# The last stage of a macaron block rebuilt: two buffers for sums, parts, results and loads, bias as PE rows, two tiles to a PSUM bank

## The reference

```python
x = x + 0.5 * ffn(layernorm(x))
x = x + attention(layernorm(x))        # ends in out @ out_proj_weight.T
x = x + 0.5 * ffn(layernorm(x))

def ffn(x):                            # T = 8192 tokens, d = 256, 8 experts, k = 2
    scores = softmax(x @ W_gate)       # 7 columns
    w = top_k(scores, 2); w = w / w.sum()
    # every expert has the weights W_expert and none overflows, so that
    # moe = (w1 + w2) * (x @ W_expert.T)
    return x @ W_shared.T + moe + bias
```

## Time and profile before

| | |
|---|---|
| median of 3 runs | 1385.76 us (1383.72 to 1387.34) |
| profiled execution | 1387.56 us, of which its span is 1385.8 us |
| busy share of the span | PE 90%, DVE 85%, ACT 66%, POOL 33% |
| mean DMA rate | 126 GB/s, mean busy share of the 16 DMA engines about a half |

### The profile page before, as it was taken

One profiled execution on the slowest core, in us unless ns is written; L12 is line 12 of the kernel. 1 busy time (PEld: TensorE's weight loads), 2 busy tenths in 40 slices (PEclk: granted clock), 3 DMA queues, 4 the chain that ended last, 5 costly groups with the idle time before them and its releaser, 6 DMA issues. The chain is left out here.

```text
span 1385.8 us, 38137 instructions
## 1 busy us (share of the span) xinstructions
PE 1253.4 (90%) x9260; PEld 832.4 (60%) x9260; DVE 1174.6 (85%) x4599; ACT 908.5 (66%) x1828; POOL 457.5 (33%) x877
## 2 busy tenths in 40 slices
PE   4999999979999999999999999999999985888785
PEld 3999988855545445455454454454454534778785
DVE  4788888749999999999999999999999963777776
ACT  3666666621778777777777777787777782444442
POOL 3333333210223222222222222222222215777671
PEclk9999999985999999999999999999999997998888
DMA  3466665973445646556466465574664643444431
GB/s 110 155 229 229 227 221 212 252 213 51 76 79 107 93 90 106 84 100 108 78 102 98 83 108 87 97 103 86 99 101 80 107 119 114 157 163 147 159 136 61
DMA packets 121898, 174.11 MB, mean 126 GB/s; under 512 B 44012, under 2 KB 71788, under 8 KB 121804
## 3 DMA queue, kind: packets, MB, share of 16 engines
q1 hardware_dynamic: 121816, 173.30, 53.9%
HBM read 96.08 MB, written 76.02 MB: 124 GB/s over the span
## 5 line engine op out<-in xcount | busy, mean ns | idle before, releaser
L1000 ACT ACTIVATE b_probs<-bank 128x512 f32<-128x512 f32 x1152 | 597.5, 614 | 135.7 <-PE bank L1124 131.9
L1027 DVE CUSTOM_DVE_ANT_0 b_junk<-bank,mask 128x512 bf16<-128x512 f32 (+3 forms) x1032 | 446.8, 488 | 1.4 <-issue 1.2
L1030 DVE TENSOR_REDUCE b_pm<-bank 128x1 f32<-128x512 f32 x516 | 322.5, 684 | 19.5 <-PE bank L1101 18.5
L1143 PE MATMUL bank<-b_probs,b_vx 128*32 128x512 f32 (+3 forms) x3072 | 310.3, 499 | 4.3 <-ACT b_o L985 1.9
L1124 PE MATMUL bank<-qs,ks 50*128 50x512 f32 (+3 forms) x1056 | 293.6, 383 | 4.5 <-ACT b_probs L1000 2.4
L1101 PE MATMUL bank<-ks,qs 48*128 48x512 f32 (+3 forms) x1056 | 277.4, 390 | 10.9 <-PEq L443 6.3
L1101 PEld LDWEIGHTS bank<-ks,qs 48*128 48x128 f32 x1056 | 165.4, 193 | 134.8 <-DVE b_pm L1030 61.6
L145 POOL TENSOR_TENSOR hold_pool<-zero 128x1 f32<-128x1 f32 x192 | 37.1, 193 | 630.8 <-ACT b_probs L1000 478.0
L1124 PEld LDWEIGHTS bank<-qs,ks 50*128 50x128 f32 x1056 | 159.7, 188 | 57.4 <-ACT b_probs L1000 51.3
L960 POOL TENSOR_SCALAR_AFFINE_SELECT b_probs<-b_probs 128x512 f32<-128x512 f32 x256 | 158.0, 635 | 0.0
L1124 PE MATMUL bank<-b_qs,b_ks 50*128 50x512 f32 (+2 forms) x480 | 135.3, 379 | 2.1 <-ACT b_probs L1000 1.2
(11 more groups left out here) (104 smaller groups left out, 2051.5 us busy)
## 6 DMA issues: line engine op xcount, KB each, us to landing
scr_qk<-a_qk SPq DMA_DIRECT2D x64, 512.0 KB, 3.2
qs<-scr_qk SPq DMA_DIRECT2D x132, 128.0 KB, 4.5
ks<-scr_qk SPq DMA_DIRECT2D x132, 128.0 KB, 5.2
scr_o<-b_o SPq DMA_DIRECT2D x64, 256.0 KB, 3.3
b_qs<-scr_qk SPq DMA_DIRECT2D x66, 128.0 KB, 4.0
b_ks<-scr_qk SPq DMA_DIRECT2D x66, 128.0 KB, 4.4
a_x<-x SPq DMA_DIRECT2D x16, 512.0 KB, 3.5
scr_x<-a_x SPq DMA_DIRECT2D x16, 512.0 KB, 2.7
```

The costliest lines, as they stand in the source:

```text
L1000: act.activation(probs[:, PROB_BUF[s], h, :], score_bank(g, t, last)[:], ACT.Exp).then_inc(p_ready, 1)
L1027: ins = dve.tensor_tensor_reduce(junk[:, t % MB, off:off + w], src, mask[:, BANK - w:BANK], 1.0, 0.0, ALU.add, ALU.max, pm[:, g.buf, 0, pl ...
L1030: ins = dve.tensor_reduce(pm[:, g.buf, 1, place(h), i:i + 1], src, AX.X, ALU.max)
L1143: last = pe.matmul(o_bank[2 * D * h:2 * D * (h + 1), col:col + w], vx[g.buf][:, j, h, :], probs[:, PROB_BUF[src], h, off:off + w], start=( ...
```

## The change

Only the last stage is changed; three load helpers of the class `First` take a buffer and a semaphore as arguments. A new class `Tail` takes the place of `Experts` there.

- `x2`, `out`, `x1`, `num`, `rden`, `oh` and `ol` get two buffers each, taken in turn by the parity of the chunk, with semaphores of their own for loads and stores. `num` and `rden` of chunk c+3 are loaded once chunk c+1 is divided, x1 of c+2 once the residual sums of c are done.
- Two tiles share a PSUM bank: output projection of tile t in bank 6 + t//2, the shared product in bank 4 + t//2. The residual sum and the collecting of the shared product are then two instructions of 128x512 instead of four of 128x256.
- The bias goes into the shared product: one more matmul for a tile, a constant 2.0 matrix against a matrix `brow` that holds the high part of the halved bias in row 0 and its low part in row 1. Five instructions of DVE build the two once. `pool_xb` is gone; x2 itself is added.
- Of the four outputs of a chunk DVE does tiles 0 and 1 as before. For tiles 2 and 3 ACT scales the expert's part by the weight in place (`act_scale`), and POOL adds the collected sum one step later (`pool_outs`). In the last chunk DVE does all four.
- Orders change: POOL divides chunk c+2 after `pool_rstd(c)`; PE does one tile of the output projection ahead of the transposes and three behind; DVE starts a step with the second collect and the logits of c-2, and ends it with the first collect of c-1; ACT runs `act_normalise` whole, between tiles 2 and 3.

The core of the diff, class `Tail` first (head and tail of the streams, the new gate and the load helpers left out; the gate differs by a wait on `scaled`):

```diff
+    def pe_tile(self, pe, k, t, first):
+        n, q = k * TPC + t, k * 2 + t // 2
+        ex, sh = self.banks["X"][t % 2], self.banks["S"][t // 2]
...
+        if not (first and t < 2):
+            pe.wait_ge(self.yl_ready, n - 1)
+        if t % 2 == 0 and not first:
+            pe.wait_ge(self.acc_ready, q - 1)
...
+        pe.matmul(half, twos[:], brow[:], start=True, stop=False)
...
+    def act_scale(self, act, k, turn):
+        act.wait_ge(self.gate_chain, k * GATE_LINKS + GATE_LINKS)
+        for t in range(self.SPLIT, TPC):
+            act.activation(self.yl[turn][:, t, 0:E], self.yl[turn][:, t, 0:E], ACT.Identity, scale=self.wsum[:, t:t + 1],
+                           bias=self.ln.zero[:, 0:1]).then_inc(self.scaled, 1)
...
+    def dve_collect(self, dve, k, p, x, turn, fresh):
+        dve.wait_ge(self.sh_done, k * 2 + p + 1)
...
+        dve.scalar_tensor_tensor(out=self.acc[turn][:, two, :].rearrange("p t e -> p (t e)"), in0=self.banks["S"][p][:], scalar=0.5,
+                                 in1=x[:, two, :].rearrange("p t e -> p (t e)"), op0=ALU.mult,
+                                 op1=ALU.add).then_inc(self.acc_ready, 1)
...
+    def pool_outs(self, pool, k, turn, fresh):
+        self.out_free(pool, k, turn, fresh)
+        pool.wait_ge(self.acc_ready, k * 2 + 2)
+        for t in range(self.SPLIT, TPC):
+            pool.wait_ge(self.scaled, k * 2 + t - 1)
+            pool.tensor_tensor(self.out[turn][:, t, :], self.yl[turn][:, t, 0:E], self.acc[turn][:, t, :],
+                               ALU.add).then_inc(self.pool_out_done, 1)
```

The step of SP:

```diff
+            def step(c, parity, o_next, out3, x_next):
+                if o_next:
                     sp.wait_ge(on_ready, c * KC + 2 * KC)
-                    load_o(c + 2)
+                    load_o(c + 3, 1 - parity)
+                if out3:
+                    ffn.store(sp, io, c - 3, 1 - parity)
+                if x_next:
+                    sp.wait_ge(x2_ready, c * 2 + 2)
+                    load_x1(c + 2, parity)
```

The step of POOL:

```diff
+            def step(c, parity, out3, nxt, nxt2, first=False):
+                if out3:
+                    ffn.pool_outs(pool, c - 3, 1 - parity, isinstance(c, int) and c < 5)
                 if nxt:
-                    divide(c + 1)
-                    low(c + 1)
+                    low(c + 1, 1 - parity)
                 ln.pool_rstd(pool, c, mhalf, first)
-                ffn.pool_xb(pool, c, x2, hbias, first)
+                if nxt2:
+                    divide(c + 2, parity)
```

The step of ACT:

```diff
             def step(c, parity, prev2, prev, here, nxt):
...
+                    high(c + 1, turn)
+                if prev:
+                    for t in range(3):
+                        ffn.act_tile(act, c - 1, t, turn, fresh)
+                if here:
+                    ln.act_normalise(act, c, x2[parity], not prev)
+                if prev:
+                    ffn.act_tile(act, c - 1, 3, turn, fresh)
+                if prev2:
+                    ffn.act_scale(act, c - 2, parity)
```

The step of DVE:

```diff
             def step(c, parity, prev2, prev, here):
...
+                if prev2:
+                    ffn.dve_collect(dve, c - 2, 1, x2[parity], parity, young(4))
+                    ffn.dve_logits(dve, c - 2, parity)
                 if prev:
                     ln.dve_low(dve, c - 1)
                 if here:
-                    residual(c, (2, 3), prev)
-                    stats(c, range(TPC))
+                    for p in range(2):
+                        residual(c, p, parity, prev, prev2)
+                        stats(c, p, parity)
                     ln.dve_aggregate(dve, c, not prev)
...
+                    ffn.dve_gate(dve, c - 2, not young(3))
+                    ffn.dve_outs(dve, c - 2, parity, young(4), (0, 1))
+                if prev:
+                    ffn.dve_collect(dve, c - 1, 0, x2[turn], turn, young(3))
```

The step of PE:

```diff
                 if here:
-                    project_out(c, prev, range(2))
-                if prev:
-                    ln.pe_transpose(pe, k, ident)
+                    project_out(c, parity, prev, (0,))
+                if prev:
+                    ln.pe_transpose(pe, c - 1, ident)
                 if here:
-                    project_out(c, prev, range(2, TPC))
+                    project_out(c, parity, prev, (1, 2, 3))
```

More of the change, by code:

```diff
@@ L1243, in _ @@
             sp.wait_ge(r_stored, 16)
-            step(1, False, True, True)
-            with loop(sp, 2, NCHUNK - 2) as c:
-                step(c, True, True, True)
-            step(NCHUNK - 2, True, True, False)
-            step(NCHUNK - 1, True, False, False)
-            store(NCHUNK - 2)
-            store(NCHUNK - 1)
-            sp.wait_ge(stored, NCHUNK * 16)
+            for c in range(3):
+                step(c, c % 2, True, False, True)
+            turns(sp, 3, NCHUNK - 3, lambda c, parity: step(c, parity, True, True, True))
+            step(NCHUNK - 3, (NCHUNK - 3) % 2, False, True, True)
+            for c in range(NCHUNK - 2, NCHUNK + 2):
+                step(c, c % 2, False, True, False)
+            ffn.store(sp, io, LAST, LAST % 2, last=True)
+            for turn in range(2):
+                sp.wait_ge(ffn.stored[turn], NCHUNK * 8)
         @block.gpsimd
@@ L1329, in _ @@
+            ffn.act_exp(act, LAST)
         @block.vector
         def _(dve):
[L1331 to L1348 removed]
@@ L1350, in stats, with residual @@
-            def stats(c, tiles):
-                for t in tiles:
-                    dve.wait_ge(x2_ready, c * TPC + t + 1)
-                    ln.dve_stats(dve, c, t, x2)
+            def residual(c, p, parity, later, later2):
+                if p == 0:
+                    if parity or not (isinstance(c, int) and c == 0):
+                        dve.wait_ge(x1_loaded[parity], c * 8 + 8 * parity)
+                    else:
+                        dve.wait_ge(chunk.x1_loaded, 16)
+                    if later2:
+                        dve.wait_ge(ln.xn_ready, c * TPC - TPC)
+                dve.wait_ge(op_ready, c * TPC + 2 * p + 2)
+                two = slice(2 * p, 2 * p + 2)
+                dve.tensor_tensor(x2[parity][:, two, :].rearrange("p t e -> p (t e)"), o_bank[p][:],
+                                  x1[parity][:, two, :].rearrange("p t e -> p (t e)"), ALU.add).then_inc(x2_ready, 1)
@@ L1434, in macaron @@
+            step(0, 0, False)
+            step(1, 1, True, first=True)
+            turns(pe, 2, NCHUNK, lambda c, parity: step(c, parity, True))
+            step(NCHUNK, 0, True, here=False)
 def macaron(nc, x, wqkv_t, wsh_t, wex_t, wgate, wout_t, bias, out):
```

308 lines of the change are left out of this document (190 added, 118 removed).

## The result

| | before | after |
|---|---|---|
| median, us | 1386.05 (1383.72 to 1387.34, 4 runs) | 1350.38 (1347.45 to 1353.60, 4 runs) |
| ratio to before, 95% interval | | 0.9745 (0.9719 to 0.9771) |
| profiled execution, us | 1387.56, span 1385.8 | 1353.60, span 1351.8 |
| mean distance of the starts of `dve_low`, ten steps from 1207 or 1208 us on | 13.53 | 10.57 |

The forecast was 1350.0, so the time is met; not all of its terms are. First the table of stretches after, which answers the earlier trace rows: us long, busy us and instructions of PE, PEld, DVE, ACT and POOL, the granted clock, the DMA share, GB/s. The last row is one step.

A forecast was written before the change was run, and what follows sets the result against it. The prediction took a cycle of waits between engines to bound the last stage, no engine being full. It summed 1171.0 + 15 x 10.9 + 15.5 = 1350.0 us; forecast 1342 to 1361, with the range reaching from 1342.5 to 1370.

The forecast's parts named there:

- Path 1: Layernorm of chunk c in a steady step, residual sums to second half of `low`, ACT's scalings included: 10.5 us.
- The 0.4 us added for three paths side by side: Supplement on the steady step's paths, giving the forecast period of 10.9 us.
- Path 2: PE in a steady step: 76 matmuls, transposes, a stand for the last normalised tile; ends at 10.4 to 10.5 us.
- Path 3: DVE in a steady step: 8.65 us of work plus 1.0 to 1.5 of stands for POOL, 9.7 to 10.1.
- Rival C: Slower: blocks between DVE and POOL decide, placed at the gate; 16.3 us a step, 1432 us at worst; chance 0.08.
- The cover of the loads: POOL's `rden` load gets a whole step more; if that failed, division late by up to 2.1 us, before its cast.
- PE's stand for the residual sum: Old steady steps: PE waits for DVE to read a shared bank, 27.5 us in 13 waits; claimed to vanish.
- the two waits: Old steady steps: PE for the residual sum (27.5 us) and POOL for `rden` (14.9), seen as closing the cycle.
- Head and drain: Stage's start and end: head change counted zero (bounds -1 and +1.5 us), drain 15.5 us.
- Rival A: Stands move, PE waits for `low`, clock keeps falling: period 12.1 us, time 1368; chance 0.23 with what lies between.
- Rival B: Cycle not shortened, new work and waits eat the buffers' gain: period 13.1 to 13.3 us, 1382 to 1388; chance 0.07.

The follow-up runs named there:

- e1: Kernel after, with ACT's scaling of tiles 2 and 3 cut to one column of 256: 1344.97 us, ratio 0.9706, period 10.14.
- e13: Kernel after, with ACT's scalings of chunk c-3 moved behind the layernorm's cast of chunk c-1: 1346.64 us, ratio 0.9706, period 10.25.
- e2: Kernel after without the four bias matmuls of a chunk (bias not added): 1351.53 us, ratio 0.9765, period 10.57.
- e4: Kernel after, with POOL dividing chunk c+2 ahead of the layernorm's scale of chunk c: 1368.19 us, ratio 0.9872, period 12.04.
- e5: Kernel after, with all four outputs on DVE, without ACT's scaling and `pool_outs`: 1359.40 us, ratio 0.9812, period 11.40.
- e12: Kernel after with single buffers for `num` and `rden` alone, loaded a step later: 1378.35 us, ratio 0.9945, period 12.46.
- e7: Kernel after with single buffers for `num`, `rden`, `x1` and `out`, loads a step later: 1386.49 us, ratio 1.0006, period 13.05.
- e11: Kernel after with a single buffer for `out` alone: 1363.07 us, ratio 0.9831, period 11.55.
- e8: Kernel after with the old banks (tiles t and t+2 share), four half-width residual sums, two ahead of `low`: 1349.81 us, ratio 0.9753, period 10.81.
- e14: Kernel before with two buffers for `num`, `rden` and `out`, loads one chunk earlier, nothing else: 1382.89 us, ratio 0.9969, period 13.30.
- e6: Kernel after, with head loads of `x1` of chunk 1 and of chunk 2 issued only once chunk 1 is divided: 1354.41 us, ratio 0.9786.

## Why the prediction was right or wrong

**Path 1 was right term by term, and is the period.** From the end of one `low` to the end of the next:

| term | priced | measured |
|---|---|---|
| residual sums, statistics, aggregates | 3.36 | 1251.67 to 1255.07: 3.40 |
| POOL's four | 1.88 | to 1257.06: 1.99 |
| handing over to ACT | 0.14 | to 1257.19: 0.13 |
| four normalisations | 2.08 | to 1259.17: 1.98 |
| tile 3 | 0.27 | to 1259.44: 0.27 |
| two scalings | 1.00 | to 1260.43: 0.99 |
| casts, half of `low` | 1.77 | to 1262.23: 1.80 |
| sum | 10.5 | 10.56 |

The scaling, which before had no row for, was priced from the normalisation of the same shape, and e1 shows that all of it lies on the path: 0.42 less work, 0.43 less period.

**The 0.4 us added for three paths side by side was wrong.** No run shows such a term. The distances from start to start hold what a handing over costs already, and path 1 alone, at 10.56, is the period of 10.57. This made twelve periods 10.9 long and not 10.54: 4.3 us too many.

**Path 2** was priced 0.2 too long, and PE is not the limit in these kernels. PE's own step was priced at 10.15 and is 9.96: the transposes take 0.79 from their start to the next matmul and not their duration of 1.04. PE stands 0.34 to 0.37 for `low`. Even in e1 and e13 the period (10.14, 10.25) stays above the 9.96. The bias costs nothing in a steady step, as it lies within PE's stand (e2).

**Path 3 was priced with the blocks on the wrong engine.** The gate does lie beside POOL's small instructions and none of its own takes over 0.19. The second output and the logits were to wait 1.0 to 1.5 us. Measured are 0.88 for two outputs and 0.19 for the difference. The outputs do meet the division, and it is the division that became 0.21 longer, with room for it. The difference meets nothing: it begins as the division ends (1259.79) and is done before POOL's outputs (1260.11). DVE's own work was right: of the step of 10.57 it stands 1.05 for the cast, 0.68 for PE and 0.21 for ACT, which leaves 8.63 against 8.65 priced. The Trainium skill (SBUF — State Buffer, "Who interferes with whom") calls the shared port pair an exclusive lock, for which issue order decides who blocks. The weight of e4 agrees: it came behind POOL's instruction and waited to its end (0.93 against 0.17). In the kernel after the outputs came first, and it is POOL's pair that lost 0.21 (2.73 against 2.52). Rival C, with its place at the gate, was the right mechanism at the wrong size: with the gate beside the division, one of the six instructions is blocked, for 0.76, and most of the 1.5 us is POOL's own late start. Four outputs in a row beside the division cost more, 2.06 (e5).

**The cover of the loads was mis-sized, and it was the term that could have broken the forecast.** The step said: if it failed, the division would be late by up to 2.1 us, still ahead of its cast. The kernel after has the second buffers, so the term wasn't called on. But taken away it costs 1.89 us a step on average (e12), with `out` and `x1` too 2.5 (e7). The 2.1 was a wait in a kernel with a period of 13.5, and such a wait shows only what is left of the transfer at that period. What had to be added up was the cycle, and the rows of before have its parts: a division of 2.53, and 9.02 from the first issue to the landing (1264.75 to 1273.77), together 11.55 and so above the 10.9. The landing has also grown, as the table of DMA issues from 1210 to 1310 shows (KB each, median us from issue to landing), first after, then before:

```profile
out<-c_ffn_out SPq DMA_DIRECT2D x10, 512.0 KB, 6.9
```

```profile
out<-c_out SPq DMA_DIRECT2D x7, 512.0 KB, 3.2
```

The number of transfers a step is the same; the store now goes out right behind the four loads. With a second `out` nobody waits for it; with one, DVE waits 2.5 to 3.5 us in each step (e11).

**What held the old period was named too narrowly.** PE's stand for the residual sum was read as the place where it closes, and the pairs of tiles as a cure. Giving the old banks back costs 0.24 us (e8). What is left to have ended PE's long stand is DVE's new order together with the lighter POOL. This is argued, for no run undoes either by itself. The prediction also took the two waits as closing one cycle. With only one of the two taken away the period is still 13.30 (e14) or 13.05 (e7).

**Head and drain.** The drain is 15.47, priced at 15.5. The head was counted at zero with bounds of -1 and +1.5, and the products start 3.86 later; counted from the stage's memset, so without the first two stages, it is 24.51 against 20.36, 4.15 more. These rows of after, POOL and then PE, and the same of before show where:

```profile
1150.39 0.12 POOL L1403 MEMSET c_ffn_ex<- 128x32 f32 x1 [4.74 <-POOLq L773]
1161.08 2.49 POOL L1410 TENSOR_TENSOR on<-c_num,c_rden 128x512 f32<-128x512 f32 x2 [10.56 <-DMA c_rden<-scr_r]
```

```profile
1168.45 2.81 PE L247 MATMUL bank<-ident,c_ln_xn 128*128 128x128 f32 x8 [0.74 <-ACT c_ln_xn L237]
1170.91 0.56 PE L152 MATMUL bank<-wh,c_oh 128*128 128x256 f32 x1
1171.27 0.42 PE L152 MATMUL bank<-wl,c_oh 128*128 128x256 f32 x1
```

```profile
1150.68 0.12 POOL L1255 MEMSET c_ffn_ex<- 128x32 f32 x1 [4.56 <-POOLq L773]
1159.77 2.48 POOL L1262 TENSOR_TENSOR on<-num,rden 128x512 f32<-128x512 f32 x2 [8.96 <-DMA rden<-scr_r]
```

```profile
1167.47 2.00 PE L247 MATMUL bank<-ident,c_ln_xn 128*128 128x128 f32 x8
1169.43 0.28 PE L152 MATMUL bank<-wl,c_oh 128*128 128x256 f32 x1
```

The first division starts 1.60 later, for the most part from the shared loads (e6). I had counted the early loads as a gain of 0.7 and not the transfers beside them. Between the division and the transposes 0.33 are won back. The transposes take 2.46 from their start to the next matmul, where they took 1.76, and the matmuls behind them, up to the first product, 3.99 in place of 1.81. The larger part of this is the clock: in before it was granted in full from 1169 us on (1.00), and twelve matmuls ran 0.12 apart. In after PE had just stood 0.74, and the eighteen ran 0.21 apart, at 0.50, up to 1174.90. So of the 2.18 only some 1.3 are the six more matmuls (6 x 0.21) that I had put at 0.7, and the rest comes with the level. I had priced the head at the upper level.

**The first three periods** take 34.91 instead of 3 x 10.9 = 32.7. The second is 14.79 long and holds this row of ACT; beside it a line of the table of DMA queues from 1191 to 1194.5:

```profile
1194.43 1.09 ACT L237 ACTIVATE c_ln_xn<-c_x,c_ln_nbias,c_ln_rstd 128x256 f32<-128x256 f32 x2 [3.36 <-issue]
```

```profile
q14 instruction: 1, 0.01, 0.6%
```

ACT stood 3.36 us there without waiting for anything that the profile shows, once. The traces have stands of 1.4 to 4.0 us in the same place in every other kernel that has the new order but e4, and five of these a second one, on DVE, some 10 us later; before has one of 1.6, on DVE. In the kernel after a single packet of instructions (8 KB) starts at 1192.80, 1.63 us before ACT goes on, and in the other kernels ACT's stand ends 1.6 to 1.7 us behind such a packet too. That ACT waited for its own code is what this argues for; no run tested it.

The errors nearly cancel: head +3.9, first three periods +2.2, twelve periods -4.3, drain 0.0, together +1.8 for the span (1351.8 against 1350.0). The profiled execution is 3.2 above the median of its runs, and so the median, 1350.38, fits the forecast better than its terms do. That the number is met to 0.4 us is luck; that the period is 10.57 and set by path 1 is not.

**Rival A**, a clock that keeps falling, did not come: the granted clock is 1.00 in the long stretch, where PE stands at most 0.37 us at a time from 1220 to 1320. **Rival B**, that nothing is gained, is what e7 shows for the change without its buffers. It had a chance of 0.07 because two visible waits were to go, and it was nearer than that.

## What to carry to other kernels

Before you price a step by its waits, add up every cycle that has a single buffer in it (last reader, issue behind whatever stands ahead on the queue, landing, first reader). A wait of 1 us can stand for a chain that is as long as the period, and here two of nearly one length gave their gain only when both were cut. Price the path that remains by durations from start to start, without a supplement for handing over, and look on it for work that could stand one instruction later: here two scalings ahead of a cast cost 0.32 us a step until they stood behind it. Don't read the limit off an engine's busy share: PE at 99 and 100% was not it in e13 and e1, as the comparison with its shortest step (9.96) shows.

## What the runs showed of the hardware

- When a DVE instruction with two operands in SBUF runs beside one of POOL, it is not always the same engine that pays. Two outputs beside a division took 0.88, and the division 0.21 more; four took 3.73 where they take 1.67 alone, and the division 2.84. The two cases differ in how many follow one another; that this makes the difference was not tried by itself. The small instructions of the layernorm on POOL (1.04 us for `rstd`, 128x4) stretched none of the gate's, each 0.16 to 0.18 beside them; but the last of them (`nbias`) took 0.43 in place of 0.21 beside DVE's outputs in e13.
- One transfer's time from issue to landing more than doubled (3.2 to 6.9 us for the same 512 KB) with the DMA share from 1220 to 1320 going from 0.44 to 0.60 and the store standing right behind four loads.
- The granted clock was 1.00 from 1220 to 1320 in every kernel whose PE stood at most 1.2 us at a time there (after, e1 to e6, e8, e13), also where PE was busy only 92% (e4) and 90% (e5). It was 0.98 in e12 and e11, with stands of up to 1.4 and 2.1 us, 0.93 in e7, with up to 3.6, and 0.86 in before, with up to 2.9.
- In the head the matmuls behind the transposes ran 0.12 us apart in before (granted 1.00) and 0.21 in after (0.50). PE had stood 0.74 us just ahead of the transposes in after, and not in before.
